# A transformer decoder on one core: two small TensorE steps of the second layer cut into four column tiles

## The reference, cut to what the change touches

Two post-norm decoder layers on `x` of 8 sequences x 512 tokens x 256 channels, all in fp32. Layer 0 is linear attention, cross attention and a quantized feed-forward. Layer 1, in which the change lies, is a causal "metric" attention without softmax, a cosine cross attention with a learned null key, and a linear step made from sparse Fourier weights. Each step is added to `x` and normalized.

## Time and profile before

| | |
|---|---|
| runs shown | 1371.81, 1372.87, 1374.49 us, median 1372.87 |
| the profiled execution, first to last instruction | 1374.7 us |
| PE busy | 1243.7 us (90%), 7340 matmul records |
| PE weight loads | 828.6 us (60%) |
| DVE busy | 1048.2 us (76%) |
| ACT, POOL busy | 517.7 us (38%), 267.8 us (19%) |
| chain that ended last, by engine | PE 74%, DVE 16%, DMA 3%, ACT 3%, issue 2%, POOL 1% |
| `met_state` matmuls, L1282 | 96 records, 12.1 us busy |
| `cos_norm`'s null logits, L1371 | 32 records, 15.0 us busy |

### The profile page before, as it was taken

How to read it: one execution, slowest core, us unless ns; L and a number is a source line. 1 busy time by engine, 2 the same in 40 slices (tenths; PEclk the granted TensorE clock), 3 DMA queues, 4 the chain that set the end, 5 groups by cost and what they waited for, 6 DMA issues and landing times.

```text
span 1374.7 us, 18473 instructions
## 1 busy us (share of the span) xinstructions
PE 1243.7 (90%) x7340; PEld 828.6 (60%) x7340; DVE 1048.2 (76%) x1966; ACT 517.7 (38%) x608; POOL 267.8 (19%) x194
## 2 busy tenths in 40 slices
PE   7899999997999999853779999999999999998976
PEld 4566666665644554321566776767768686766654
DVE  3578899986634789998564787969878797887777
ACT  1244334433534567587013323232322333231421
POOL 0011111112100000033100413204132141413242
PEclk9899999999999999976899999999999999999998
DMA  5001000102582045489322011100211000000000
GB/s 219 16 16 32 31 1 31 32 16 93 150 295 77 31 153 185 167 315 373 107 87 84 31 54 62 54 31 32 63 54 54 32 24 21 27 20 36 1 16 16
DMA packets 47829, 107.86 MB, mean 78 GB/s; under 512 B 10752, under 2 KB 31360, under 8 KB 44288
## 3 DMA queue, kind: packets, MB, share of 16 engines
q1 hardware_dynamic: 43584, 104.59, 21.7%
q10 hardware_dynamic: 4160, 2.10, 0.5%
HBM read 62.64 MB, written 44.04 MB: 78 GB/s over the span
## 4 chain that ended last, share of the span: by engine, by line
PE 74%; DVE 16%; DMA 3%; ACT 3%; issue 2%; POOL 1%; SPq 0%; POOLq 0%; ACTq 0%; DVEq 0%
PE ps L1357 8%; PE ps L1420 7%; PE ps L1236 6%; PE ps L1067 6%; PE ps L1118 4%; PE ps L817 4%; PE ps L1393 3%; PE ps L1302 3%; PE ps L965 2%; PE ps L890 2%; PE ps L1326 2%; PE ps L1337 2%; PE ps L1467 2%; DMA arena<-up_scratch 2%; PE ps L908 2%
## 5 line engine op out<-in xcount | busy, mean ns | idle before, releaser
L1420 PE MATMUL ps<-arena 128*128 128x256 f32 x512 | 120.1, 389 | 5.8 <-ACT arena L1892 5.8
L1357 PE MATMUL ps<-arena 128*128 128x512 f32 x256 | 117.6, 598 | 0.0
L1420 PEld LDWEIGHTS ps<-arena 128*128 128x128 f32 x512 | 98.6, 195 | 27.9 <-ACT arena L1892 9.9
L2535 DVE TENSOR_TENSOR arena<-ps,arena 128x2048 f32<-128x2048 f32 x32 | 73.3, 2292 | 38.1 <-PE ps L1302 37.9
L1938 POOL TENSOR_TENSOR arena<-arena 128x4 f32<-128x4 f32 x44 | 45.5, 1038 | 282.0 <-DVE arena L2124 282.0
L1998 POOL TENSOR_TENSOR arena<-arena 128x16 f32<-128x16 f32 x32 | 92.2, 2916 | 32.5 <-DVE arena L2564 32.5
L1236 PE MATMUL ps<-arena 128*128 128x256 f32 x384 | 88.2, 386 | 5.2 <-DVE arena L2456 5.2
L1067 PE MATMUL ps<-arena 128*128 128x512 f32 x192 | 83.8, 593 | 1.2 <-ACT arena L1620 1.2
L1118 PE MATMUL ps<-arena 128*128 128x512 f32 x192 | 84.4, 594 | 0.0
L1236 PEld LDWEIGHTS ps<-arena 128*128 128x128 f32 x384 | 73.0, 194 | 16.5 <-issue 7.0
L1357 PEld LDWEIGHTS ps<-arena 128*128 128x128 f32 x256 | 46.2, 190 | 48.7 <-issue 45.1
(11 more groups left out here) (311 smaller groups left out, 2651.9 us busy)
## 6 DMA issues: line engine op xcount, KB each, us to landing
v_scratch<-arena SPq DMA_DIRECT2D x7, 1536.0 KB, 12.9
arena<-v_scratch SPq DMA_DIRECT2D x7, 1536.0 KB, 6.8
up_scratch<-arena SPq DMA_DIRECT2D x6, 1536.0 KB, 6.0
arena<-up_scratch SPq DMA_DIRECT2D x6, 1536.0 KB, 12.6
vw_scratch<-arena SPq DMA_DIRECT2D x32, 256.0 KB, 3.8
arena<-x_scratch SPq DMA_DIRECT2D x16, 512.0 KB, 4.7
arena<-vw_scratch SPq DMA_DIRECT2D x8, 1024.0 KB
arena<-x SPq DMA_DIRECT2D x8, 512.0 KB, 5.7
```

The source lines that it names most:

```text
L1357: last = mm(flat(p % 2), w["cos_wq"][:, k, p * P:(p + 1) * P], xt4[:, k], start=k == 0, stop=k == NC - 1)
L1420: last = mm(flat(2)[:, C:2 * C], cos_pt[:, p], cos_vw[:, par, p], start=p == 0, stop=p == NP - 1)
L2535: v.tensor_tensor(met_s[:, n % 2].rearrange("p r t h n -> p (r t h) n"), flat(3, 4).rearrange("p (h n) -> p h n", n=P), w["causal"].unsque ...
```

```diff
@@ met_state
                 for c in range(NC):
                     for t in range(NT - 1):
-                        rows = met_pr[:, t, c * P:(c + 1) * P]
-                        last = mm(flat(5 + c)[:, t * P:(t + 1) * P], rows, rows, start=True, stop=True)
+                        for g in range(4):
+                            rows = met_pr[:, t, c * P + 32 * g:c * P + 32 * g + 32]
+                            at = (c * (NT - 1) + t) * 32
+                            last = mm(flat(5)[32 * g:32 * g + 32, at:at + 32], rows, rows, start=True, stop=True)
@@ cos_norm
                         mm(flat(2)[32 * j:32 * j + 32], w["head_sel"][:, e], cos_sq[2 * j + e],
-                           start=e == 0, stop=e == 1 and j > 0, skip_group_check=True)
+                           start=e == 0, stop=False, skip_group_check=True)
                 for k in range(NC):
-                    last = mm(flat(2)[0:32], null_wq[:, k], xt4[:, k],
-                              start=False, stop=k == NC - 1, skip_group_check=True)
+                    for t in range(NT):
+                        last = mm(flat(2)[32 * t:32 * t + 32, t * P:(t + 1) * P], null_wq[:, k],
+                                  xt4[:, k, t * P:(t + 1) * P],
+                                  start=False, stop=k == NC - 1, skip_group_check=True)
@@ met_mask_states
-                n = (NT - 1) * P
+                n = NC * (NT - 1)
                 link(v.tensor_tensor(
-                    met_st, bank(5, 2)[:, :, 0:n].rearrange("p c (t n) -> p c t n", t=NT - 1),
-                    w["blk16"].unsqueeze(1).unsqueeze(1).broadcast_to([P, NC, NT - 1, P]), ALU.mult))
+                    met_st.rearrange("p c t (g n) -> p (c t) g n", g=4),
+                    flat(5)[:, 0:32 * n].rearrange("p (a n) -> p a n", a=n).unsqueeze(2).broadcast_to([P, n, 4, 32]),
+                    w["blk16"].rearrange("p (g n) -> p g n", g=4).unsqueeze(1).broadcast_to([P, n, 4, 32]), ALU.mult))
@@ cos_floor
-                v.tensor_copy(cos_nn[:, :, H:], nn[:, :, 0, 4:4 + H]).then_inc(sig("cos_floored").sem, 1)
+                nulls = flat(2, 2)[:, 0:NT * (P + 32)].rearrange("p (t n) -> p t n", t=NT)
+                v.tensor_copy(cos_nn[:, :, H:], nulls[:, :, 4:4 + H]).then_inc(sig("cos_floored").sem, 1)
```

## The result

The changed kernel takes 1355.27 us (median of four runs, 1354.22 to 1360.19), the kernel before in the same job 1373.68 (four runs, 1371.81 to 1376.75): a ratio of 0.9864, interval 0.9844 to 0.9885. Faster, as forecast, but by more: on the 1372.87 us that the prediction started from, the ratio gives 1354.2 where 1358.2 was predicted, and that lies just under the low end of the range. So there are two questions: did the two edits save what the sum says, and where do the other 3 to 4 us come from? (One execution of the kernel before, at 1876.6 us and a mean granted clock of 0.65, is left out of all comparisons here.)

What follows compares the result with a forecast made beforehand. PE was taken to bound the kernel, busy for 77.61 of 79 us in a middle step; 9.7 us from the null logits plus 5.0 from the states, 14.7 off the median 1372.87, gave 1358.2 us, range 1355 to 1365.

Steps and rivals of the forecast that it cites:

- the sum: Whole kernel: 9.7 us from the null logits plus 5.0 us from the states, 14.7 us less.
- Edit 1: Null logits in `cos_norm`, cut into four column tiles: 1.26 us a sequence less, 0.89 in the last, 9.7 in all.
- DVE's floor behind it: DVE's L2562 behind the null logits: waits 1.87 us for PE, so it can start 1.26 us sooner.
- POOL's root: POOL's L1998 behind L1938, last sequence: on the path, can come only 0.89 us sooner instead of 1.26.
- take the gain back: Rival at L2562: DVE could not start sooner, PE would wait 1.26 us more at L1407; 1367.9 us, chance 0.06.
- Edit 2: States in `met_state` as 48 passes of 32 columns replacing 12 of 128: 0.63 us a sequence less, 5.0 in all.
- changes of shape: PE's array around `met_state` changes shape twice more, entering and leaving column tiles: costs 0.29 us a sequence.
- The rival of 0.109 us a group: In `met_state`, 32-column groups pace no faster than 128-column ones: 7.6 us gained in total, 1365.3 us, chance 0.17.
- the one of isolated groups: In `met_state`, each group waits for its loads and matmuls, some 0.4 us a group: slower, 1393 us, chance 0.03.
- Theory two: Posed after the measurement, whole kernel: the edits by themselves gain more than the summed 14.7 us; no chance given.

Runs made afterwards that it cites:

- this edit alone: Only the null logits by quarters, states as before, against the kernel before: 1360.78 us, ratio 0.9905; second time 1364.96 us, ratio 0.9947.
- edit 2 alone: Only the states as 32x32 blocks, null logits as before, against the kernel before: 1367.2 us, ratio 0.9952; second time 1367.3 us, ratio 0.9963.

## Why the prediction was right in its mechanism and short in its size

**Edit 1: right.** The pace of 0.109 us for four tiles of 128 columns (0.44 us for 16 passes), 1.26 us a sequence (1.25 with this edit alone), DVE's floor behind it, and POOL's root that caps the last sequence: each stands in the rows above. DVE did not take the gain back: 0.61 us of its wait are left, as 1.87 - 1.26 said.

**Edit 2: right.** Pace 0.035, measured 0.033; changes of shape 0.29, measured 0.26 to 0.29; gain 0.63, measured 0.64 alone. The floor of about 25 ns from start to start in the Trainium skill ("TensorE: Matmul & The Clock Gate", section "Wait — 56ns, not 53.3ns?") does not carry over to passes that take turns in four column tiles: 8 ns a pass for 48 further ones. The rival of 0.109 us a group and the one of isolated groups fall with the same row.

**The sum: right.** A full middle step is 1.87 to 1.90 us shorter in every pair of traces, and 1.89 was summed. That the whole stretch of the first pair came to 14.76 us against 14.7 is luck in part: over four traces each it is 15.2, and what goes beyond the sum is chiefly slow matmuls in the first step.

**The step that failed** is the one from the sum to the time: "the runs shown spread by 1.1 to 1.6 us about their median, and in the last stretch the mean clock is 0.93, so a spell at the lower level, 1.2 GHz, can fall a little otherwise there: I go down to 1355." The term was seen, given 2.5 us at the low end of the range (1357.5 to 1355), and put at nothing in the forecast. The rows to price it were in the trace of before: 1.65 and 5.89 us for matmuls that take 1.09 and 3.72 elsewhere, 2.73 us on the path. Over four traces each, the tail is 27.2 us before (28.1, 25.4, 28.1, 27.0) and 25.4 to 25.5 after: 1.7 us on average, and taking the spell away from the kernel before alone gives 1.8, with a standard error of 0.7 and an interval of the ratio that just reaches 1. With the stretch that makes 15.2 + 1.7 = 16.9 us for the pooled 17.0 (standard error 0.6). These shares are not firm: the same eight traces also start the stretch 2.4 us sooner after the change, by spells that both kernels can have, and with that they would add up to 19.3.

The same step took three runs (1371.81 to 1374.49) for the kernel's spread; 108 executions lie between 1368.88 and 1378.0, with a mean 0.8 us above that median. And four runs of the changed kernel are few: by the means of all runs the ratio gives 1355.8 us on the same 1372.87, inside the range, so that the first result fell outside is chance in part; 1358.2 stays 2.4 us too high either way. The start of the stretch differs by up to 4.8 us between two traces of one kernel (690.90 and 686.13 before), 3.6 of it in the two slow pieces of the first stage, and the first pair of traces, which has them before and not after, makes the change look like 22.3 us.

Left open: why the tail's spell lands one output step earlier in the changed kernel. The traces fit a place that goes with the program (five of five with both edits, none of nine without), and the idle matmuls fit its price, but no run moved it on purpose in the changed kernel; a gain of this kind can go again with the next edit. Theory two is not excluded by the totals alone: the pairs with idle matmuls gave 15.9 and 13.5 us where it had 17 to 18 and 16.9, and it is the middle steps that speak most clearly against it. That the slow matmuls near 1270 us account for most of the 1.1 us in the trace of edit 2 alone was read, not tested.

## What to carry to other kernels

Where a matmul's outputs are blocks on a diagonal, or fill few rows, cutting it into column tiles pays by the columns that are no longer computed (edit 2) or that now run four tiles side by side (edit 1). Tiles alone gained nothing: the states over all 128 columns lost 0.26 us. Price it by the distance between starts, and add the change of shape at its borders (here 0.29 us against a gain of 0.92). Before a prediction of about 1% is compared with a measurement, look in the trace of before for pieces that run at the lower clock, price them by the same pieces at the upper one, and ask whether they lie on the path: such a piece is a term of the sum, because any change of timing may move it into a wait or out of one. Compare two profiles by the stretch between two marks in the program around the edit, not by their spans, and best by a step that repeats: here the whole stretch differed by 1.3 us between executions of one program, a full step by 0.02.

## What was not expected of the hardware

One program, run again, differs at the lower clock in places that nothing in it changed. Windows of the same ten microseconds, kernel before, first trace, then third:

```profile
37.00:47.00 10.00, 9.01 (x35) 7.96 (x36) 5.16 (x18) 0.67 (x1) 0.17 (x1) 0.53 0.00 1
```
```profile
37.00:47.00 10.00, 9.14 (x45) 5.94 (x45) 5.28 (x20) 0.26 (x1) 2.35 (x1) 1.00 0.00 1
```

A granted clock of 0.53 (next to the lower level, 1.2 GHz) against 1.00 (2.4 GHz), behind the same waits of PE (0.89 us at 34 us, 1.9 at 36). Which of the two it will be can be read 30 us earlier, from L767's length. The single passes of L767 show why that length differs: they have spans of 1061 ns at first and of 592 later, and the one in between starts at 10.4 us in the changed kernel's first trace, at 12.1 in the first of the kernel before and at 12.9 in the changed kernel's third. So TensorE gets fast there at another instant in each execution, although the clock's column shows 1.00 throughout. How that decides the spell 30 us later is open.

And some matmuls whose results nobody reads, in waits of one or two microseconds in the first stage and the last sequence, cut the scatter of the kernel before by more than half (2.6 to 1.1 us) without costing it time. In the last sequence alone they left it at 2.4, which points to those of the first stage; no run has them there alone.
